# Attention and mixture-of-experts kernel: weight chunks split one unit sooner, centroids split ahead of the loop

## The reference

```python
x = x + cross_attention(layernorm(x), ctx)      # 16 heads of 8; softmax over axis 1, the HEADS
x = x + moe(layernorm(x))

def moe(x):                                     # per token
    raw = x @ centroids.T                       # 8 experts
    top2 of sigmoid(raw + routing_bias); gates = softmax(sigmoid(raw)[top2])
    h = gelu(x @ Wfc.T); y = h @ Wproj.T        # 2 shared experts, 8 routed, hidden 512
    return x + sum(shared y) + sum(gate * y of the two chosen experts)
```

## Time and profile before

| | |
|---|---|
| median of 3 runs | 389.18 us (387.49 to 391.11) |
| the profiled execution | 387.26 us, of which the span from first to last instruction is 385.5 us |
| mean granted PE clock | 0.962 of full speed |
| busy share of the span | PE 86%, DVE 71%, ACT 68%, POOL 68% |

### The profile page before, as it was taken

One profiled execution on the slowest core, in us unless ns is written; L12 is line 12 of the kernel. 1 busy time (PEld: TensorE's weight loads), 2 busy tenths in 40 slices (PEclk: granted clock), 3 DMA queues, 4 the chain that ended last, 5 costly groups with the idle time before them and its releaser, 6 DMA issues.

```text
span 385.5 us, 11809 instructions
## 1 busy us (share of the span) xinstructions
PE 331.7 (86%) x4100; PEld 272.6 (71%) x4101; DVE 274.6 (71%) x592; ACT 263.7 (68%) x498; POOL 260.3 (68%) x268
## 2 busy tenths in 40 slices
PE   4777687598989879999999898899999999999253
PEld 1563365476777668888887676798998989999253
DVE  3879999997989969906756446677676776776246
ACT  2886999478696747574536787576776667767746
POOL 6354698789998682777777773077777777777600
PEclk9996999789999999999999999999999999999858
DMA  7956344310000000111114611323243232331098
GB/s 251 342 158 265 102 129 130 100 40 3 2 4 2 2 2 7 51 57 48 56 50 125 100 54 49 91 67 87 66 108 93 67 87 75 81 94 49 2 352 304
DMA packets 29179, 36.16 MB, mean 94 GB/s; under 512 B 4932, under 2 KB 24007, under 8 KB 28624
## 3 DMA queue, kind: packets, MB, share of 16 engines
q1 hardware_dynamic: 24592, 27.13, 23.5%
q0 software_dynamic: 4544, 8.44, 7.0%
HBM read 21.74 MB, written 14.72 MB: 95 GB/s over the span
## 4 chain that ended last, share of the span: by engine, by line
PE 34%; issue 18%; DVE 18%; POOL 16%; DMA 6%; ACT 6%; POOLq 1%; SPq 1%; DVEq 0%; ACTq 0%
POOL results L518 7%; PE banks L1499 5%; DVE Mx L929 4%; POOL gathered L500 4%; DVE Z L943 3%; POOL E L446 3%; ACT E L642 2%; PE banks L1483 2%; PE banks L1599 2%; PE banks L1484 2%; PE banks L1485 2%; PE banks L1601 2%; PE banks L1585 2%; PE banks L1603 2%; PE banks L1586 2%
## 5 line engine op out<-in xcount | busy, mean ns | idle before, releaser
L518 POOL DMA_INDIRECT results<-E,qRep x78 | 86.1, 1104 | 42.3 <-issue 27.4
L500 POOL DMA_INDIRECT gathered<-xs,slot x64 | 64.7, 1011 | 25.7 <-issue 18.3
L1224 DVE TENSOR_TENSOR E<-hid,E 128x512 f16<-128x512 f32 x78 | 54.0, 692 | 36.3 <-ACT E L783 36.3
L446 POOL TENSOR_TENSOR E<-E,rZ 128x1024 f32<-128x1024 f32 x32 | 67.6, 2133 | 13.4 <-DVE rZ L946 13.3
L781 ACT ACTIVATE hid<-banks 128x512 f32<-128x512 f32 x78 | 47.0, 602 | 38.2 <-DVE E L1224 22.6
L1599 PE MATMUL banks<-wprojL,E 128*128 x312 | 54.6, 219 | 2.9 <-DVE E L1224 1.9
L1603 PE MATMUL banks<-wprojH,E 128*128 x312 | 54.3, 219 | 0.0
L1601 PE MATMUL banks<-wprojH,E 128*128 x312 | 54.2, 219 | 0.0
L783 ACT ACTIVATE E<-banks 128x512 f16<-128x512 f32 x78 | 47.3, 606 | 0.0
L642 ACT ACTIVATE E<-banks 128x1024 f32<-128x1024 f32 x32 | 33.1, 1090 | 18.6 <-PE banks L1356 18.6
L1585 PE MATMUL banks<-qRep,wfcH 128*128 128x256 f16 x156 | 42.6, 273 | 0.9 <-ACT E L783 0.5
(11 more groups left out here) (227 smaller groups left out, 868.5 us busy)
## 6 DMA issues: line engine op xcount, KB each, us to landing
qRep<-gathered SPq DMA_DIRECT2D x39, 129.0 KB, 2.2
qRep<-q_rows SPq DMA_DIRECT2D x32, 128.0 KB, 2.5
qRep<-results SPq DMA_DIRECT2D x8, 512.0 KB, 7.4
X<-in_x SPq DMA_DIRECT2D x4, 512.0 KB, 6.3
q_rows<-qRep SPq DMA_DIRECT2D x8, 256.0 KB, 2.1
out<-X SPq DMA_DIRECT2D x8, 256.0 KB, 3.2
results<-E,qRep POOLq DMA_INDIRECT x78
gathered<-spare SPq DMA_DIRECT2D x9, 129.0 KB, 4.4
```

What stands on the lines that cost most here:

```text
L446: g.tensor_tensor(heads, heads, rZ[:, k % 2, :].unsqueeze(1).unsqueeze(3).broadcast_to([P, HH // 2, P, 2]), ALU.mult).then_inc(attn_ready, 1)
L500: g.indirect_dma_start(out=gathered, out_offset=bass.IndirectOffsetOnAxis(ap=slot[:, k, i:i + 1], axis=0), in_=xs[:, i, :], in_offset=None ...
L518: g.indirect_dma_start(out=results, out_offset=bass.IndirectOffsetOnAxis(ap=xg[:, k, h, 2 * D:ROW].bitcast(I32), axis=0), in_=yg[:, k, h, ...
L1224: v.tensor_tensor(gL[:, j, 2 * c:2 * c + 2], hid[:, 2 * j + c].rearrange("p (c q) -> p c q", c=2), gH[:, j, 2 * c:2 * c + 2], ALU.subtract ...
```

## The change

`WEIGHT_UNITS` places chunk (4, 1) in unit 5 instead of 6, chunks (4, 2) and (4, 3) in unit 6 instead of 7, and nothing in unit 7. `split_centroids` is called once ahead of the first `four_units` of DVE instead of within unit 1. No instruction is added or removed.

```diff
-WEIGHT_UNITS = ((), ((3, 0),), ((3, 1),), ((3, 2),), ((3, 3),), ((4, 0),), ((4, 1),), ((4, 2), (4, 3)))
+WEIGHT_UNITS = ((), ((3, 0),), ((3, 1),), ((3, 2),), ((3, 3),), ((4, 0), (4, 1)), ((4, 2), (4, 3)), ())
...
-                    if first and k == 1:
-                        split_centroids()
                     if k == 3 and not first:
                         deviation_seed(n - 1, not second)
...
+            split_centroids()
             four_units(0, True, False)
             four_units(1, False, True)
```

## The result

Over 22 runs of each the change takes 387.26 us in the median and the kernel before 389.89. The ratio is 0.9936, 95% interval 0.9914 to 0.9958: 2.5 us less (1.6 to 3.4). It leaves out the runs that took over 1.5% longer than the fastest of their kernel, so it isn't exactly the quotient of the two medians. The difference lies within the 1% that I had said a measurement of this kernel can't tell from no change; this many runs tell it. I had forecast 0.8 us less, so the sign and the range held and the size was a third of the measured one.

The account below looks back on a forecast made before the run. DVE was taken to bound units 2 to 5, with ACT's unit 7 work and then POOL on the path. Centroid and chunk gains less the seed's delay came to 0.8 us: 389.18 to 388.4 us, range 386.0 to 391.2.

Parts of the forecast that it names:

- The path in unit 7: ACT's chunks in unit 7 delay exps(8); without them 85.6 against 86.65, and the second inverse root 0.8 us sooner.
- part 1: Centroid split moved from unit 1 to ahead of the first unit: 0.4 us gained of 1.45 removed, cost 0.
- The seed behind the second chunk: Unit 7 on DVE: half_var waits for POOL's second chunk, so the seed comes 0 to 1.15 us later, 1.15 taken.
- rival 1: half_var wins the port at the boundary, so the seed costs nothing: 387.6 us, chance 0.27.
- one chunk less in its full stretch: POOL, from the first inverse root to unit 9's normalise: one chunk less, 1.15 us, net -0.5 there.
- The centroids: Unit 1 on DVE: 1.45 us removed, only 0.4 taken as usable because ACT sits right behind DVE.
- Rival 2: Another wait in units 9 to 12, POOL late with normalise(7) or (9), takes up the gain: 389.2 us, chance 0.16.
- Rival 3: PE's lower clock lasts over half_sum and minus_max ahead of unit 8, costing 2.95 us: 391.3 us, chance 0.12.

Follow-up runs that it names:

- e3: The change, but POOL does its low parts in the old units (5: one, 6: one, 7: two), ACT's stay early; ratio 0.9924.
- e4: The change, but POOL does chunk (4, 1) behind the inverse root of unit 5 instead of ahead; ratio not told from the change's.
- e8: The change, with POOL's chunk (4, 0) behind unit 5's inverse root, (4, 1) and (4, 2) in unit 6, (4, 3) in unit 7; ratio 0.9947.
- e10: The change, unchanged, profiled again on another, slower chip; ratio 0.9845, with widely spread runs.
- e9: The kernel before, unchanged, run again on another chip, where it takes 471.9 us.
- e12: The kernel before plus small unread matmuls where PE idled, on the other chip; 46.96 us from max_heads(0) to max_heads(7).
- e11: The change plus small unread matmuls where PE idled (units 0, 1, 6, 7), on the other chip; ratio 0.9968.
- e6: The kernel before, with split_centroids moved from behind to ahead of max_heads(1), still inside the loop; ratio 0.9951.
- e1: The change with the old WEIGHT_UNITS, so only the centroids move; ratio 0.9944.

## Why the prediction was right, and where its size was off

**The path in unit 7.** Right: `exps(8)` forecast for 85.6 came at 85.61, `max_heads(9)` forecast for 88.25 came at 88.25, `normalise(7)` forecast from 89.0 came at 88.82, and the second root, forecast 0.8 sooner, came 0.9 sooner. Counted from `max_heads(7)` that is 0.5, which L13 confirms in five runs. Wrong: the sentence "So ACT's work in unit 7 is on the path". `exps(8)` and `max_heads(9)` do come sooner with it, but e3 gives that back by `max_heads(13)`; ACT's work there is on the path only as far as it lets POOL do its chunk earlier. Part of this agreement in moments is luck: the forecast had taken 0.4 off for part 1, and in the profile 1.35 less in L7 and a start 0.95 late make 0.4 as well.

**The seed behind the second chunk.** Right in mechanism: `half_var` took 1.08 us (0 to 1.15 forecast, 1.15 taken), and rival 1, that it gets in at the boundary, did not happen. Its time of 387.6 is near the measured 387.26, for another reason. But I charged the delay to `exps(8)` as if it were on the path, and e4 shows that `normalise(6)` covers it up to `max_heads(9)`.

**POOL.** Right in mechanism: one chunk less in its full stretch was in the sum, and e3 shows that the weights' gain comes by way of POOL. The size is in part luck. The sum's own terms give 0.65 - 1.15 = -0.5, of which 0.4 is part 1, so that 0.1 is left for the weights; the 0.8 was a choice between 0.5 and 1.0. Counted from `max_heads(7)` the first root came 0.89 later (1.05 forecast without part 1) and the stretch behind it is 1.39 shorter (1.15 forecast); the idle time of 0.22 that POOL had ahead of `normalise(9)` went with the chunk.

**The centroids.** Here the size failed. The step, in the prediction's words, was "Of the 1.45 us removed not all is usable, since ACT sits right behind DVE", with the value "I take 0.4, the nearest row". The idle time of 0.43 ahead of `exps(2)` is room, but not all of it. Two more amounts bear on it, the room behind ACT and PE's clock. `exps(2)` of before ends at 45.87 and the second half of the raw scores of unit 3 is ready at 46.36, while `max_heads(3)` starts at 46.66: 0.3 behind ACT. PE, then DVE, in the kernel before:

```profile
45.92 0.44 PE L1347 MATMUL banks<-qRep,kRep 32*64 32x128 f16 x16 [0.25 <-ACT E L642]
```

```profile
46.66 2.28 DVE L929 TENSOR_REDUCE Mx<-banks 128x128 bf16<-128x2048 f32 x1
```

With 0.43 that makes 0.73, and e8, whose PE clock was low in unit 1 for as long as in before, is 0.78 shorter in L7 (46.94 to 46.16). The remainder goes with PE's clock. In the profile before PE was at its lower level (1.2 GHz) in unit 1, and `exps(1)` therefore late, at 9.61 behind `max_heads(0)` instead of 8.61 in e10. The windows of before, then of the change's second profile, e10:

```profile
33.00:35.00 2.00, 2.00 (x20) 0.81 (x12) 1.64 (x1) 2.00 (x5) 1.30 (x2) 0.50 0.96 394
35.00:37.00 2.00, 2.00 (x9) 1.27 (x8) 1.97 (x3) 0.71 (x2) 2.00 (x2) 0.50 0.35 134
```

```profile
34.00:36.00 2.00, 1.89 (x28) 0.95 (x16) 1.71 (x1) 2.00 (x5) 1.15 (x2) 1.00 0.98 400
36.00:38.00 2.00, 1.04 (x4) 0.31 (x4) 2.00 (x2) 1.47 (x3) 2.00 (x3) 1.00 0.38 144
```

The centroid wait lay on top of this late `exps(1)` and hid it, so that ACT looked closer to DVE than it is when PE's clock is up. Without the centroid wait the late `exps(1)` shows, in e8: DVE idles for PE, and the step from `max_heads(1)` is 6.38 instead of 5.94.

```profile
40.08 2.29 DVE L933 TENSOR_REDUCE Mx<-banks 128x128 bf16<-128x2048 f32 x1 [0.37 <-PE banks L1350]
```

Pairs of profiles with PE's clock low in unit 1 for as long give the same order: 0.78 with `exps(1)` at 9.61 (before, e8), 1.29 at 9.11 and 9.12 (e9, e3), 1.67 at 8.63 (e12, e11). With the clock up the centroids are worth up to 1.69 (e10; e4 has the same L7), more than the 1.45 of their own rows: the step from `max_heads(0)` to `(1)` is 5.62 there against 5.85 before. In the kernel before such a quicker start is lost again (e12: 5.64, then 7.62 instead of 7.38), as `centL` ends with POOL's chunk in any case. With 0.5 of the weights that is 1.3 to 2.2 us. The measured 2.5 (1.6 to 3.4) agrees with the upper part within its interval; what the last 0.3 is, if it is anything, stays open. How often each case occurs, over many executions, no run here shows; that the clock's low stretches come less often in the change is possible and was not tested.

**Rival 2.** The gain was not taken up by POOL or another wait: L13 fell by what was computed.

**Rival 3.** The mechanism exists: in e11 the low level reached into `half_sum(7)` and cost 1.4 us. In the change it ended before `half_sum(7)`, which takes 2.08 us at 82.10 as before, and the granted clock from 78 to 95 us is 0.91 against 0.94. It does not decide, since the stretches move from execution to execution and strike both kernels.

## What to carry to other kernels

A tiny VectorE instruction that takes 1 us in the trace and ends where a GpSimd instruction ends is a wait, not work: move it to where GpSimd stands still (e6: a few instructions further up in the same loop, 1.44 us less in that step, no other change). Room between two engines is the idle time ahead of the second plus the room behind it, read at the place where the first one is due again; taking the first idle time alone was the mistake here. And where an engine is full over a stretch, look at when the stretch ends: the relief of another engine (e3) and an earlier start with more work inside (e8) moved waits about and gave nothing by then, while one piece of work less inside gave 0.5 us.

## What was not expected

- The stretches at PE's lower level fall at different places in executions of the same or nearly the same program, and whether one costs anything depends on what lies over it: nothing in unit 1 before, 1.2 us in unit 2 of e1, 1.6 us after the attention in the change's profile. With small matmuls in PE's idle times one such stretch still fell on costly work (e11).
- One chip takes 82 us more for the same kernel (471.9 against 389.9), all of it behind the attention units, while L7 is 46.94 us on both.
